# Keys of the next batch ahead of the values, and the value copy and loads at the head of ScalarE's next step, in the attention stage of a gated layer

## The chip, the core and the metric

The kernel runs on one core of a Trainium2 chip. The metric is the device time of one execution in microseconds; lower is better. Engines: PE is TensorE (PEld its weight loads), DVE is VectorE, ACT is ScalarE, POOL is GpSimd, SP is SyncE. SPq, ACTq and POOLq in the rows are the same engines' queues issuing DMA transfers.

## The reference

Two residual blocks. The first is a decayed linear attention with rotary factors, the second a two-of-eight mixture of experts whose weights each have a low-rank correction.

```
q, k, v = LN(x) @ Wq, ctx @ Wk, ctx @ Wv            # 8 batches of 256 x 256
q, k = xpos(q), xpos(k)                             # rotary, with a scale
ret  = (q @ k.T) * decay_mask
x    = x + tanh(g_xattn) * (ret @ v)
xf   = LN(x)
gates = top-2 of softmax(xf @ Wg.T), normalised
y_e  = (silu(xf @ (W1 + A1 B1) + b1) * (xf @ (W3 + A3 B3) + b3)) @ (W2 + A2 B2) + b2   # 8 experts
x    = x + tanh(g_ffn) * sum_e gates_e * y_e
```

## The kernel before

All engine programs are written out by hand, each in the order in which its engine runs it; semaphores join them. There are two stages. The first runs eight steps, one per batch of 256 rows, and the change lies in it. The second works through 39 tiles of 128 gathered rows, one expert each, and its matmuls follow one another with hardly a gap.

In step `s` of the first stage three things are interleaved. For batch `s`: the key, query and value projections, their rotation, the layer norm of the input rows. For batch `s-1`: scores, the masked product with the values, the residual, the second layer norm. For batch `s-2`: the expert logits and the two largest. Beside them the weights of expert `s-1` are made ready: `unit(s-1, ., m)`, m = 0 to 5, is a sixth of the low-rank product on PE, `add` puts it on a staged sixth of the weight on DVE, `weight_hi` (`hi(m)`) rounds that on ACT into WH, and `weight_lo` on POOL writes the rest into WL, which frees the staging buffer for SP's next load.

The names that the steps below use:

- PE `step`: the key product into `pK`; transposes of `xn2` (normalised rows of batch `s-2`); `scores(s)`; `units(0, 1)`; `logits(s-2)`, which wait for ACT's copy `xn2T`; `attend`, which waits for DVE's masked `ret` and for the copy `v`; transposes of `xn`; `units(2, 3)`; the query product, which waits for ACT's copy `xnT`; the value product into `pV`; `units(4, 5)`.
- DVE `step`: rotation of the keys in two products (`tA`, `tB`), the variance between them; then a reciprocal (`rs`) that waits for ACT's square root `sd` of that variance; shift, mask, adds 0 and 1, the two largest, residual, adds 2 and 3 and the second norm between them; rotation of the queries; sums of the next rows; adds 4 and 5.
- ACT `step`: copy `xn2T`, square root `sd`, normalised rows `xn`, `hi(0, 1)`, copy `xnT`, `hi(2)`, second square root, `hi(3)`, normalised rows `xn2`, value copy `v`, two DMA stores (`out`, `xn_rows`), two DMA loads by `next_batch(s+2)` (rows `xs`, context `cx`), `hi(4, 5)`, and in steps 1 to 3 a store of low-rank factors (`lora_parts`).

The rows `xs` have three buffers, the context `cx` two. The context buffer is read by the key product and by the value product of its batch, so its reload stands behind a wait for the value product on ACT.

Of the kernel before, what the change touches and what calls it, by code (L numbers as in the profile page):

```python
# [31 lines left out]
ACT = mybir.ActivationFunctionType  # L32
# [3 lines left out]
B, S, D = 8, 256, 256  # L36
# [44 lines left out]
def flamingo(nc, x, ctxT, wqkv, tables, mask, gates_in, w_all, lora, biases, wgT, ident_in, consts, out):  # L81
# [9 lines left out]
    with whole:  # L91
# [379 lines left out]
        def _(pe):  # L471
# [9 lines left out]
            def unit(s, u, m):  # L481

                kind, n = m // 2, s * UNITS + m
                lb, before = ls_of(s, kind)
                if m % 2 == 0:
                    pe.wait_ge(s_ls[lb], 3 * 16 * (s + 1 if lb == kind else E + 1))
                pos_wait(pe, s_add, n - 1)
                L = LS[lb]
                if kind < 2:
                    c = m % 2  # L490
                    last = nc.tensor.matmul(pW[m % 2][:, :], L[:, c * P:(c + 1) * P], L[:, D:LCOL], start=True, stop=True)
                else:
                    for h in range(2):
                        c = 2 * (m % 2) + h
                        last = nc.tensor.matmul(pW[m % 2][:, h * D:(h + 1) * D], L[:, c * P:(c + 1) * P], L[:, HID:LCOL],
                                                start=True, stop=True)
                last.then_inc(s_unit, 1)
# [36 lines left out]
                nc.tensor.matmul(pO[:, D:2 * D], ret[:, 2 * P:3 * P], vv[:, 1, :], start=False, stop=True  # L534
                                 ).then_inc(s_out, 1)

            def step(s, u, two, three):
                def units(*ms):
                    if two:
                        for m in ms:  # L540
                            unit(s - 1, 1 - u, m)

                pe.wait_ge(s_ctx[u], 16 * (half(s, u) + 1))
                pos_wait(pe, s_krot, s)
                for m in range(2):
                    for c in range(CH):
                        last = nc.tensor.matmul(pK[:, m * S:(m + 1) * S], wq[:, 1, c, m * P:(m + 1) * P], cx[u][:, c, :],
                                                start=(c == 0), stop=(c == CH - 1))
                last.then_inc(s_kproj, 1)
                if three:  # L550
                    pe.wait_ge(s_xn2, s - 1)
                    transposes(xn2, s_xn2Tp)
                if two:
                    scores(s)
                units(0, 1)
                if three:
                    pe.wait_ge(s_qrot, s)
                    logits(s - 2, pL)
                if two:
                    attend(s, v[1 - u])  # L560
                else:
                    pe.wait_ge(s_vtab, 2 * 16)
                if three:
                    pe.wait_ge(s_xn2T, s - 1)
                pe.wait_ge(s_xn, s + 1)
                transposes(xn, s_xnTp)
                units(2, 3)
                if not two:
                    pe.wait_ge(s_tab, 4 * 16)
                pe.wait_ge(s_xnT, s + 1)  # L570
                pos_wait(pe, s_qrot, s)
                pos_wait(pe, s_L, s - 1)
                for m in range(2):
                    for c in range(CH):
                        last = nc.tensor.matmul(pQ[:, m * S:(m + 1) * S], wq[:, 0, c, m * P:(m + 1) * P], xnT[:, c, :],
                                                start=(c == 0), stop=(c == CH - 1))
                last.then_inc(s_qproj, 1)

                pos_wait(pe, s_v, s)
                for t in range(TPB):  # L580
                    for c in range(CH):
                        last = nc.tensor.matmul(pV[:, t * D:(t + 1) * D], cx[u][:, c, t * P:(t + 1) * P], wq[:, 2, c, :],
                                                start=(c == 0), stop=(c == CH - 1))
                last.then_inc(s_vproj, 1)
                if s == B - 1:
                    ranks(1, pK, trimA, onesA, HA, HSA)
                units(4, 5)

            def ranks(n, dst, tri, ones, H, HS):

# [133 lines left out]
        def _(act):  # L724
# [25 lines left out]
            def weight_hi(s, u, m):  # L750
                act.wait_ge(s_add, s * UNITS + m + 1)
                nc.scalar.activation(w_dst(WH, s, m), stage[stage_of(s * UNITS + m)][:, :], ACT.Copy).then_inc(s_wh, 1)  # L752
# [18 lines left out]
            def next_batch(t, u):  # L771

                r = t % XRING
                pos_wait(act, s_x2, t - XRING + 1)
                act.dma_start(xs[r][:] if r < 2 else xs[r], x[t]).then_inc(s_xload[r], 16)
                act.dma_start(cx[u][:], ctxT[t]).then_inc(s_ctx[u], 16)

            def store_rows(b):

                rows = bass.ds(b * S, S)  # L780
                act.wait_ge(s_x2, b + 1)
                act.wait_ge(s_xn2, b + 1)
                if b < B - 1:
                    act.dma_start(out_rows[rows, 0:D].rearrange("(t p) d -> p t d", p=P), x2[:]).then_inc(s_store, 16)
                act.dma_start(xn2_d[rows, 0:D].rearrange("(t p) d -> p t d", p=P), xn2[:]).then_inc(s_store, 16)
# [13 lines left out]

            def step(s, u, two, three):  # L800
                hi = lambda *ms: [weight_hi(s - 1, 1 - u, m) for m in ms]
                if three:
                    act.wait_ge(s_xn2Tp, s - 1)
                    copy_xn2T(pT)
                act.wait_ge(s_mv1, s + 1)
                nc.scalar.activation(sd1[:], mv1[:, :, 1], ACT.Sqrt, bias=eps_t[:]).then_inc(s_sd1, 1)
                act.wait_ge(s_nm1, s + 1)
                pos_wait(act, s_xnTp, s)
                normal(xs[s % XRING], rs1, nm1, xn, s_xn)
                if two:  # L810
                    hi(0, 1)
                if three:
                    first_two(s - 2)
                act.wait_ge(s_xnTp, s + 1)
                nc.scalar.activation(xnT[:].rearrange("p c t -> p (c t)"), pT[:, :], ACT.Copy).then_inc(s_xnT, 1)
                if s == 0:
                    round_factors()
                    pair_factors()
                if s == B - 2:
                    act.wait_ge(s_cst, 16)  # L820
                    act.wait_ge(s_lstore, 3 * 16)
                    nc.scalar.activation(trimA, cst[:, C_TRI:C_TRI + P], ACT.Copy, scale=1.0, bias=-1.0).then_inc(s_fixed, 1)
                    nc.scalar.activation(onesA, cst[:, C_TRI:C_TRI + P], ACT.Copy, scale=0.0, bias=1.0).then_inc(s_fixed, 1)
                    nc.scalar.activation(HA, cst[:, C_TRI:C_TRI + P], ACT.Copy, scale=0.0, bias=0.0).then_inc(s_fixed, 1)
                    nc.scalar.activation(F9, cst[:, C_E:C_E + E + 1], ACT.Copy, scale=0.0, bias=0.0).then_inc(s_fixed, 1)
                    nc.scalar.activation(c5, cst[:, C_E:C_E + E], ACT.Copy, scale=float(SPARE), bias=float(SPARE)).then_inc(s_fixed, 1)
                    nc.scalar.activation(kj1, cst[:, C_HI:C_HI + KJ], ACT.Copy, scale=float(P), bias=float(P)).then_inc(s_fixed, 1)
                if s == B - 1:
                    nc.scalar.activation(slots_x, cst[:, C_IOTA:C_IOTA + P].unsqueeze(2).to_broadcast([P, P, KQ]), ACT.Copy
                                         ).then_inc(s_grid, 1)  # L830
                if two:
                    hi(2)
                    deviation(s - 1)
                    hi(3)
                    if s == B - 1:
                        act.wait_ge(s_dl, 1)
                        nc.scalar.activation(e2A, dlA, ACT.Exp).then_inc(s_e2, 1)
                        act.wait_ge(s_e2, 1)
                        nc.scalar.activation(denA, e2A, ACT.Copy, scale=1.0, bias=1.0).then_inc(s_e2, 1)
                    act.wait_ge(s_nm2, s)  # L840
                    normal(x2, rs2, nm2, xn2, s_xn2)
                act.wait_ge(s_vproj, s + 1)
                nc.scalar.activation(v[u][:].rearrange("p t d -> p (t d)"), pV[:, :], ACT.Copy).then_inc(s_v, 1)
                if two:
                    store_rows(s - 1)
                if s + 2 < B:
                    next_batch(s + 2, u)
                if two:
                    if s < B - 1:
                        hi(4, 5)  # L850
                    if s <= 3:
                        store_factors(s - 1)
# [760 lines left out]
```

## Time and profile before

| what | value |
|---|---|
| three runs | 329.84, 327.46, 328.63 us; median 328.63 us |
| span of the profiled execution (first to last instruction) | 325.4 us |
| PE busy | 297.9 us (92%) |
| DVE, ACT, POOL busy | 248.2, 206.0, 210.8 us |
| mean granted TensorE clock | 0.975 |

The time of the profiled execution itself isn't listed apart; its span lies 3.2 us under the median of the runs, and a run's time takes in what lies around the span. Busy shares are averages over two stages with different limits; the first stage is the stretch up to about 105 us.

### The profile page before, as it was taken

To read this page: it belongs to the slowest core of one execution; us is meant where nothing else is said; L and a number is where in the kernel's file an instruction comes from. 1 tells how busy PE (TensorE), PEld (TensorE's weight loads), DVE (VectorE), ACT (ScalarE), POOL (GpSimd) and SP (SyncE) were. 2 spreads that over 40 slices of the span, in tenths; PEclk is the share of its full clock that TensorE was granted. 3 is DMA by queue.
4 is the path that set the end of the run, shared out by engine and by line. 5 is a ranking of instruction groups with operands and counts; after the bars stand their busy time and mean duration, and the time that the engine had idled before them with its cause. 6 is when DMAs were issued, how large, how long until landed. Compare 5 with 4: busy or idle time off the path is not lost. (4 is left out here: it accounts for less than half of the span.)

```text
span 325.4 us, 7435 instructions
## 1 busy us (share of the span) xinstructions
PE 297.9 (92%) x1755; PEld 230.0 (71%) x1755; DVE 248.2 (76%) x607; ACT 206.0 (63%) x486; POOL 210.8 (65%) x246
## 2 busy tenths in 40 slices
PE   7589989999997798999999999999999999999960
PEld 3468778788886656776777777777777777777740
DVE  2679879889999998697988976767776776777750
ACT  5635755766878577787675565665675665675550
POOL 2457878888893098866756656766577776666241
PEclk9799999999999699999999999999999999999996
DMA  7968997999972169567747675766533223333100
GB/s 265 391 158 240 280 297 253 294 279 278 278 244 85 17 225 296 138 201 200 205 139 206 175 187 186 175 187 197 148 56 55 52 51 66 53 45 61 20 0 0
DMA packets 30424, 54.35 MB, mean 167 GB/s; under 512 B 7232, under 2 KB 15808, under 8 KB 30112
## 3 DMA queue, kind: packets, MB, share of 16 engines
q1 hardware_dynamic: 14672, 36.10, 34.1%
q0 software_dynamic: 7488, 9.36, 16.7%
q10 hardware_dynamic: 8224, 8.42, 8.6%
q8 instruction: 17, 0.28, 0.4%
q14 instruction: 23, 0.19, 0.2%
HBM read 41.92 MB, written 10.65 MB: 162 GB/s over the span
## 5 line engine op out<-in xcount | busy, mean ns | idle before, releaser
L1079 POOL DMA_INDIRECT out<-ys,cols x39 | 64.7, 1660 | 58.4 <-DMA out<-ys,cols 33.0
L883 ACT ACTIVATE gh<-bank 128x512 fp32r<-128x512 f32 x39 | 23.4, 599 | 61.0 <-PE bank L648 61.0
L640 PE MATMUL bank<-WH,xh 128*128 x156 | 55.7, 438 | 0.1
L1056 POOL DMA_INDIRECT xg<-xn_rows,colg x39 | 40.0, 1026 | 20.5 <-POOL colg L1034 10.3
L992 POOL TENSOR_TENSOR WL<-stage,WH 128x512 bf16<-128x512 f32 x38 | 47.9, 1278 | 7.3 <-ACT WH L752 7.1
L640 PE MATMUL bank<-WH,xl 128*128 x156 | 49.0, 395 | 0.0
L640 PE MATMUL bank<-WL,xb 128*128 x156 | 47.2, 385 | 0.0
L752 ACT ACTIVATE WH<-stage 128x512 fp32r<-128x512 f32 x38 | 22.9, 628 | 17.7 <-DVE stage L1110 14.5
L640 PEld LDWEIGHTS bank<-WH,xl 128*128 128x128 f32 x156 | 29.2, 188 | 6.8 <-DVE xl L1493 0.4
L1497 DVE TENSOR_TENSOR gl<-bank,gh 128x512 fp32r<-128x512 f32 x39 | 26.9, 689 | 8.8 <-ACT gh L883 8.7
L657 PE MATMUL bank<-WH,gh 128*128 x156 | 32.0, 327 | 1.5 <-ACT gh L883 1.5
L1509 DVE TENSOR_TENSOR g<-g,h 128x512 f32<-128x512 f32 x39 | 27.1, 694 | 5.0 <-ACT h L945 1.1
L1503 DVE TENSOR_TENSOR h<-bank,BA 128x512 f32<-128x512 f32 x23 | 15.9, 691 | 19.3 <-PE bank L640 18.1
L657 PEld LDWEIGHTS bank<-WH,gh 128*128 128x128 f32 x156 | 24.0, 190 | 7.7 <-issue 2.7
L1110 DVE TENSOR_TENSOR stage<-bank,stage 128x512 f32<-128x512 f32 x38 | 24.6, 676 | 0.9 <-DMA stage<-w_all_in 0.9
L657 PE MATMUL bank<-WH,gl 128*128 x156 | 24.9, 281 | 0.4 <-DVE gl L1497 0.4
L640 PEld LDWEIGHTS bank<-WH,xh 128*128 128x128 f32 x156 | 24.0, 190 | 1.7 <-issue 0.7
L648 PEld LDWEIGHTS bank<-ident,g 128*128 128x128 f32 x156 | 19.3, 140 | 8.1 <-DVE g L1509 1.1
L887 ACT ACTIVATE gb<-gh 128x512 bf16<-128x512 f32 x39 | 24.9, 638 | 0.0
L945 ACT ACTIVATE h<-h 128x512 f32<-128x512 f32 x39 | 24.9, 638 | 0.0
L640 PEld LDWEIGHTS bank<-WL,xb 128*128 128x128 bf16 x156 | 9.0, 98 | 21.3 <-issue 21.3
L657 PE MATMUL bank<-WL,gb 128*128 x156 | 23.8, 275 | 0.0
(229 smaller groups left out, 702.2 us busy)
## 6 DMA issues: line engine op xcount, KB each, us to landing
BB<-biases_in SPq DMA_DIRECT2D x16, 640.0 KB, 4.1
stage<-w_all_in SPq DMA_DIRECT2D x38, 256.0 KB, 5.1
BA<-biases_in SPq DMA_DIRECT2D x8, 640.0 KB, 3.9
WL<-w_all_in SPq DMA_DIRECT2D x10, 256.0 KB, 4.7
LS<-WH SPq DMA_DIRECT2D x45, 48.0 KB
xn_rows<-xn ACTq DMA_DIRECT2D x8, 256.0 KB, 4.1
out<-x ACTq DMA_DIRECT2D x7, 256.0 KB, 3.1
cx<-ctxT_in ACTq DMA_DIRECT2D x6, 256.0 KB, 6.5
```

What stands on the lines that cost most here:

```text
L640: last = nc.tensor.matmul(dst[:, :], lhs[p][:, c * P:(c + 1) * P], W[:, bass.ds(e * (UNITS * UC) + (2 * kind + c) * UC, HID)], start=(part ...
L657: last = nc.tensor.matmul(pY[:, 0:D], lhs[:, c * P:(c + 1) * P], W[:, bass.ds(e * (UNITS * UC) + 4 * UC + c * D, D)], start=(part == 0 and ...
L752: nc.scalar.activation(w_dst(WH, s, m), stage[stage_of(s * UNITS + m)][:, :], ACT.Copy).then_inc(s_wh, 1)
L883: nc.scalar.activation(gh[:], pG[:, :], ACT.Copy).then_inc(s_gh, 1)
L887: nc.scalar.activation(gb[:], gh[:].bitcast(F32), ACT.Copy).then_inc(s_gb, 1)
L945: nc.scalar.activation(h1[:], h1[:], ACT.Silu).then_inc(s_silu, 1)
L992: nc.gpsimd.tensor_tensor(w_dst(WL, s, m), stage[stage_of(s * UNITS + m)][:, :], w_dst(WH, s, m).bitcast(F32), ALU.subtract).then_inc(s_wl, 1)
L1056: nc.gpsimd.indirect_dma_start(out=xg[q][:], out_offset=None, in_=xn2_d[0:JA * P, :] if i < NA else xn2_d, in_offset=bass.IndirectOffsetOn ...
L1079: nc.gpsimd.indirect_dma_start(out=out_rows, out_offset=bass.IndirectOffsetOnAxis(ap=cols[:, i:i + 1], axis=0), in_=ys[p][:], in_offset=No ...
L1110: nc.vector.tensor_tensor(stage[b][:, :], pW[m % 2][:, :], stage[b][:, :], ALU.add).then_inc(s_add, 1)
L1497: nc.vector.tensor_tensor(gl[:], pG[:, :], gh[:].bitcast(F32), ALU.subtract).then_inc(s_gl, 1)
L1509: nc.vector.tensor_tensor(g[:], g[:], h1[:], ALU.mult).then_inc(s_g, 1)
```

## The change

PE's key product becomes a function `keys`. Step 0 runs it for batch 0 at its head as before; every step but the last then runs `units(4, 5)` and the key product of the next batch between its query and its value product. On ACT the value copy of a batch and the two loads move from the end of a step to the head of the next, behind `hi(4, 5)` and the factor store and ahead of the copy `xn2T`; the loads are for the batch after the one of that step, `next_batch(s+1)`. The last step keeps its value copy and its units where they were. DVE, POOL and SP run the same programs.

```diff
-            def step(s, u, two, three):
-                def units(*ms):
-                    if two:
-                        for m in ms:
-                            unit(s - 1, 1 - u, m)
+            def keys(s, u):
 
                 pe.wait_ge(s_ctx[u], 16 * (half(s, u) + 1))
                 pos_wait(pe, s_krot, s)
...
                 last.then_inc(s_kproj, 1)
+
+            def step(s, u, two, three):
+                def units(*ms):
+                    if two:
+                        for m in ms:
+                            unit(s - 1, 1 - u, m)
+
+                if s == 0:
+                    keys(0, 0)
                 if three:
                     pe.wait_ge(s_xn2, s - 1)
                     transposes(xn2, s_xn2Tp)
...
                 last.then_inc(s_qproj, 1)
+                if s < B - 1:
+                    units(4, 5)
+                    keys(s + 1, 1 - u)
 
                 pos_wait(pe, s_v, s)
...
                 if s == B - 1:
                     ranks(1, pK, trimA, onesA, HA, HSA)
-                units(4, 5)
+                    units(4, 5)
...
+            def copy_values(b, u):
+                act.wait_ge(s_vproj, b + 1)
+                nc.scalar.activation(v[u][:].rearrange("p t d -> p (t d)"), pV[:, :], ACT.Copy).then_inc(s_v, 1)
+
...
                 hi = lambda *ms: [weight_hi(s - 1, 1 - u, m) for m in ms]
+                if two:
+                    copy_values(s - 1, 1 - u)
+                    if s + 1 < B:
+                        next_batch(s + 1, 1 - u)
                 if three:
                     act.wait_ge(s_xn2Tp, s - 1)
                     copy_xn2T(pT)
...
-                act.wait_ge(s_vproj, s + 1)
-                nc.scalar.activation(v[u][:].rearrange("p t d -> p (t d)"), pV[:, :], ACT.Copy).then_inc(s_v, 1)
+                if s == B - 1:
+                    copy_values(s, u)
                 if two:
                     store_rows(s - 1)
-                if s + 2 < B:
-                    next_batch(s + 2, u)
                 if two:
                     if s < B - 1:
                         hi(4, 5)
```

On PE, in a middle step, from the units 2 and 3 (L491) over the query product (first L575, now L580), the value product (L582, now L590), units 4 and 5 (L495) and the next key product (L547, now L543) to the transposes (L502):

```order
 L491 MATMUL bank<-LS 128x512 x2
-L575 MATMUL bank<-xnT,wq 128x256 x4
-L582 MATMUL bank<-wq,cx 128x256 x4
+L580 MATMUL bank<-xnT,wq 128x256 x4
 L495 MATMUL bank<-LS 128x256 x4
-L547 MATMUL bank<-cx,wq 128x256 x4
+L543 MATMUL bank<-cx,wq 128x256 x4
+L590 MATMUL bank<-wq,cx 128x256 x4
 L502 MATMUL bank<-ident,xn 128x128 x4
```

The value product went from the place before the units to the last place before the transposes; the units and the key product stand one product earlier.

On ACT, from the normalised rows `xn2` (the row xn<-x) at the end of step 3 to the square root `sd` at the head of step 4, in the kernel before (WL<-x_in loads rows into the third rows buffer, which lies in WL):

```order
L757 ACTIVATE xn<-x,nm,rs 128x256 x2
L843 ACTIVATE v<-bank 128x512
L784 DMA out<-x 128x2x256
L785 DMA xn_rows<-xn 128x2x256
L775 DMA WL<-x_in 128x512
L776 DMA cx<-ctxT_in 128x512
L752 ACTIVATE WH<-stage 128x512 x2
L736 DMA lora_parts<-WH 48x2304
L769 ACTIVATE xn2T<-bank 128x512
L806 ACTIVATE sd<-mv,eps_t 128x2
```

And in the changed kernel, the same stretch with the loads of the same batch:

```order
L765 ACTIVATE xn<-x,nm,rs 128x256 x2
L796 DMA out<-x 128x2x256
L797 DMA xn_rows<-xn 128x2x256
L760 ACTIVATE WH<-stage 128x512 x2
L744 DMA lora_parts<-WH 48x2304
L788 ACTIVATE v<-bank 128x512
L783 DMA WL<-x_in 128x512
L784 DMA cx<-ctxT_in 128x512
L777 ACTIVATE xn2T<-bank 128x512
L822 ACTIVATE sd<-mv,eps_t 128x2
```

The value copy and the two loads went from ahead of the two roundings (WH<-stage) to behind them and behind the factor store, right ahead of the copy `xn2T` and the square root.

## Rows read from the trace of the kernel before

**Rows 1.** Stretches, steps 5 and 6: busy PE, PEld, DVE, ACT, POOL; clock; DMA share; GB/s

```profile
66.28:78.28 12.00, 11.49 (x65) 9.72 (x63) 10.81 (x36) 7.97 (x18) 10.47 (x11) 1.00 1.02 300
78.28:89.91 11.63, 11.32 (x65) 9.80 (x64) 10.61 (x36) 8.90 (x24) 10.31 (x11) 1.00 0.90 265
```

**Rows 2.** Timeline of DVE (start, length, instruction, idle before): first reciprocal of a step

```profile
21.37 0.15 DVE L1137 RECIPROCAL rs<-sd 128x2 f32<-128x2 f32 x1
...
58.36 0.17 DVE L1137 RECIPROCAL rs<-sd 128x2 f32<-128x2 f32 x1 [0.76 <-ACT sd L806]
...
70.36 0.17 DVE L1137 RECIPROCAL rs<-sd 128x2 f32<-128x2 f32 x1 [0.73 <-ACT sd L806]
...
81.98 0.17 DVE L1137 RECIPROCAL rs<-sd 128x2 f32<-128x2 f32 x1 [0.35 <-ACT sd L806]
...
93.17 0.15 DVE L1137 RECIPROCAL rs<-sd 128x2 f32<-128x2 f32 x1
```

**Rows 3.** Timeline of ACT, from the end of step 4 into step 5

```profile
66.01 0.60 ACT L843 ACTIVATE v<-bank 128x512 f32<-128x512 f32 x1
66.07 0.42 ACTq L784 DMA_DIRECT2D out<-x  x1
...
67.05 0.57 ACTq L775 DMA_DIRECT2D xs<-x_in  x1
67.65 0.82 ACTq L776 DMA_DIRECT2D cx<-ctxT_in  x1
68.51 1.15 ACT L752 ACTIVATE WH<-WL 128x512 fp32r<-128x512 f32 x2 [1.91 <-DVE WL L1110]
69.57 0.58 ACT L769 ACTIVATE xn2T<-bank 128x512 f32<-128x512 f32 x1
70.05 0.28 ACT L806 ACTIVATE sd<-mv,eps_t 128x2 f32<-128x2 f32 x1
```

**Rows 4.** Timeline of PE, step 5: query, value, units 4 and 5, next keys, transposes

```profile
74.25 1.99 PE L575 MATMUL bank<-xnT,wq 128*128 128x256 f32 x8 [0.31 <-ACT xnT L815]
76.08 1.89 PE L582 MATMUL bank<-wq,cx 128*128 128x256 f32 x8
77.62 0.82 PE L495 MATMUL bank<-LS 128*128 128x256 f32 x4
78.28 1.89 PE L547 MATMUL bank<-cx,wq 128*128 128x256 f32 x8
80.00 0.60 PE L502 MATMUL bank<-ident,xn 128*128 128x128 f32 x4
```

**Rows 5.** Timeline of DVE: adds 4 and 5 in step 5; key rotation in step 7

```profile
78.60 1.27 DVE L1110 TENSOR_TENSOR stage<-bank,stage 128x512 f32<-128x512 f32 x2
...
91.83 0.69 DVE L1115 TENSOR_TENSOR tA<-bank,WH 128x512 f32<-128x512 f32 x1 [0.34 <-PE bank L547]
```

**Rows 6.** Timeline of ACT: other value copies and loads, in steps 0, 2 and 5

```profile
17.58 0.60 ACT L843 ACTIVATE v<-bank 128x512 f32<-128x512 f32 x1 [2.81 <-PE bank L582]
17.59 0.36 ACTq L775 DMA_DIRECT2D WL<-x_in  x1
17.98 0.45 ACTq L776 DMA_DIRECT2D cx<-ctxT_in  x1
...
42.70 1.41 ACTq L776 DMA_DIRECT2D cx<-ctxT_in  x1
...
79.03 0.52 ACTq L775 DMA_DIRECT2D xs<-x_in  x1
79.58 0.50 ACTq L776 DMA_DIRECT2D cx<-ctxT_in  x1
```

**Rows 7.** Tile view of the context buffers

```profile
DMA to landing us min/median/max: 3.3/6.4/7.5
```

**Rows 8.** DMA view: issues, count, KB each, median us to landing

```profile
cx<-ctxT_in ACTq DMA_DIRECT2D x6, 256.0 KB, 6.5
lora_parts<-WH ACTq DMA_DIRECT2D x3, 432.0 KB, 7.0
```

## The prediction

> **What bounds the kernel now.** I read the page first for the two stages, then the first stage step by step in the view of stretches, then the timelines of DVE, ACT and PE side by side through one step. The second stage is one row of matmuls and nothing of it is touched, so what the first stage gains or loses is what the kernel gains or loses. So PE has about 0.3 to 0.5 us of slack a step, and something else makes the step long.
>
> That is a loop through DVE and ACT. I measure it at the first reciprocal of a step, where DVE waits 0.73 to 0.76 us for ACT's square root [rows 2]: from 58.36 to 70.36 is 12.00 us, from 70.36 to 81.98 is 11.62, and from 21.37 to 93.17 are six loops, 71.80 us together. Read one loop backwards from 70.36 [rows 2, 3]. The square root starts at 70.05, right behind the copy xn2T (69.57), which stands behind the two roundings (68.51). ACT's engine stood idle for 1.91 us ahead of them while its queue was issuing: four DMAs from 66.07 to 68.47, that is 2.40 us, of which 0.98 (66.07 to 67.05) are the two stores and 1.42 (67.05 to 68.47) the two loads. So the loop is 7.71 us from the reciprocal to the first store (66.07 - 58.36), then 2.40 of issue, then 1.89 (68.47 to 70.36: 0.04, two roundings 1.06, copy 0.48, square root 0.31). Issue time on ACT counts fully in it.
>
> **The change, part by part.** I put the reciprocal of step 5 (70.36) at zero and lay the moved work on it.
>
> *PE.* Queries start at +3.89 (74.25), and take 1.83 to the next product; values 1.54, units 4 and 5 0.66, keys 1.72 (from start to start in [rows 4]). Now units start at +5.72, keys at +6.38, values at +8.10, and the last value matmul ends at +8.10 + 1.89 = +9.99. PE's total is unchanged, and the transposes behind start at the same +9.64. The keys 1.54 us earlier are worth little: DVE waited for them 0.34 us [rows 5], but in a loop whose reciprocal then waits for ACT anyway, except in the last (93.17 has no wait behind it).
>
> *ACT, roundings.* Stores now follow the normalised rows directly and are over at about 67.0. The roundings then wait for adds 4 and 5 alone, which end at +9.51 (78.60 + 1.27 - 70.36) [rows 5]. That removes 2.40 us of issue ahead of them and puts DVE's own row of queries, sums and adds in its place.
>
> *ACT, value copy and loads.* Both now stand between the roundings and the copy xn2T. The copy of the values itself costs nothing where loads follow: it runs on the engine while the queue issues (66.01 and 66.07 [rows 3]). But its wait counts, because what is queued behind it is the loads, the copy xn2T and the square root, for which PE's logits and DVE's reciprocal wait. Values end at +9.99, later than the roundings' release at +9.51, so the copy starts at +10.03 (0.04 behind its release, as the roundings do now), the first load at +10.09; with D for the issue of the two loads, xn2T starts at +10.13 + D, the square root 0.48 later, the reciprocal 0.31 after that. The loop becomes **10.92 + D**.
>
> In steps 1 to 3 the factor store is issued ahead of the copy as well, about 0.5 us from +9.6; it ends near +10.1, with the values, and adds 0.1 or nothing.
>
> *What is D?* Before it was 0.84 with nothing else in the queue (17.59 to 18.43), 1.05 (79.03 to 80.08), 1.42 (67.05 to 68.47); in step 2 the context load alone took 1.41, some 0.9 more than in step 5 [rows 3, 6]. The bounds are 0.84 and 1.42, with a long issue on top. The changed loads no longer come directly behind two stores, which speaks for the low end; SP's weight loads fall in the same time as they do now, which speaks against it. I take 1.1, next to the 1.05 of step 5.
>
> *The last loop* (step 6 to 7) has no loads before or after, but gains a value copy ahead of xn2T: 0 to 0.53 us (one step of two roundings), less the 0.34 that keys come earlier. It took 93.17 - 81.98 = 11.19; I take 11.4.
>
> *Sum.* Five loops of 10.92 + 1.1 and one of 11.4 make 71.5, against 71.80: 0.3 us gained, 325.1 of span for 325.4, and **328.3 us** against the median of 328.63. At D = 0.84 it is 70.2 (327.0), at 1.42 73.1 (329.9), with one long issue 0.9 more. The change takes the issue of two stores and two roundings out of the loop and puts adds, the wait for later values and the same loads in; the two are worth the same. As the three runs spread over 2.4 us, under 1% (3.3 us) can't be told from nothing.
>
> **Covers.** The loads come later against their use. The context load's issue starts about 1.4 us ahead of a step's reciprocal (its own 0.55, then 0.04, 0.48 and 0.31), and the keys that read it now start at +6.38 of that same step: 7.8 us. Landing took 3.3 to 7.5, median 6.4 [rows 7]: covered, by 0.3 in the worst row. The rows are issued first and are read only shortly ahead of adds 4 and 5 (+8.24). The stores are issued no later than before, and the roundings 4 and 5, for which POOL waits, come earlier.
>
> **Rivals.**
>
> *Keys wait for their context (slower).* In steps 1 to 3 the factor store of 432 KB (7.0 us to landing [rows 8]) now goes ahead of the loads in the same queue, where it went behind them. Four transfers of the size of the context's, 256 KB [rows 8], took about 8.0 us from the first issue to the median landing of the context (67.65 + 6.4 - 66.07), 128 KB per us; 432 more are 3.4 us. Then the context lands 11.4 us after the first store, which is issued at -4.3, so at +7.1, 0.7 late, and with the longest landing 1.8 late. PE then holds the keys, and with them the values, on which the loop hangs directly. Three loops with 0.7 to 1.8 are 2.1 to 5.4 us; I put it at 331. Against it: in its present place, last of the five and issued about with the roundings (68.51, 1.85 ahead of 70.36), the store lands 7.0 us later at some +5.2, and the bytes ahead of the last of the five are the same in any order. It decides from where a landing takes more than 7.8 us.
>
> *Long issues hit the loads.* A 1.41 like that of step 2 in two or three loops instead of one: 0.9 each, 329.5 to 331.5.
>
> *The loads don't wait for the copy (faster).* If the queue could issue a DMA while an instruction ahead of it still waits for its semaphore, the loads would be out of the loop; it would be the copy behind two roundings, +9.54 + 1.06 + 0.48 + 0.31, 11.4 us in all loops, 68.4 against 71.80: 325.2. The trace speaks against it: in step 0 the engine idles 2.81 us before the value copy, and the load behind it, which waits for nothing of its own, starts 0.01 us after the copy (17.59) and not in that idle time [rows 6]. The Trainium skill, page "Perfetto Trace Analysis", section "Per-instruction lifecycle: what the profiler-reported window actually captures", has it the other way: an ACT instruction is pushed with its semaphore wait into a wait queue and the sequencer goes on to the next one. By that rule the time is the 325.2 of this rival; the trace at 17.59 disagrees.
>
> *The change doing nothing at all* is the forecast's neighbour and not told apart from it: the orders are fixed, so it does what it says.
>
> **How the numbers follow.** Forecast (D between 0.84 and 1.42) 0.62: 328.3, own range 327.0 to 329.9. Context late 0.19: 331, half of it over 331.9. Long issues 0.12: some 330.5, rarely over 331.9. Loads free 0.07: 325.2. The range of 326.2 to 331.6 leaves out the last case and the top of the second, and takes in a bad long issue. Faster by over 1% (under 325.3): the last case and a little of the forecast's low end, 0.09. Slower (over 331.9): half of the context case and a little of the long issues, 0.13. Within 1%: 0.78.
>
> **What the profile would show.** Right: PE waits nowhere for DMA; the roundings 4 and 5 start with DVE's adds; the loads start 0.06 behind the value copy and that with the end of the value product; the reciprocal still waits for ACT, 0.8 to 1.3 us; loops of 11.8 to 12.4. Wrong: an idle row of PE's keys ended by a DMA of cx; loops of 11.4 with loads issued ahead of the copy; or issue rows of the pair well under 0.8 or over 1.5 us.

## The result

The changed kernel takes 338.2 us (median of 4 runs, 336.59 to 341.44), the kernel before 328.76 on the same chip: a ratio of 1.0286, 95% interval 1.0231 to 1.0341. It is slower by 9.4 us, where 328.3 was forecast with a range up to 331.6. Each profile below is of one execution, and some are the longest that their kernel had (341.44 us for the changed kernel, with a span of 339.6), so times and ratios are taken from the medians and the profiles are read for their first stage.

The stretches of the changed kernel between the first reciprocals of its steps, in the columns of [rows 1]: length; busy time of PE, PEld, DVE, ACT, POOL; granted clock; DMA share; GB/s.

```profile
21.70:37.11 15.41, 12.88 (x63) 10.40 (x61) 10.00 (x28) 7.86 (x15) 11.67 (x12) 0.92 0.67 179
37.11:53.30 16.19, 13.26 (x64) 10.89 (x64) 10.62 (x35) 8.28 (x17) 10.25 (x10) 0.89 0.83 234
53.30:68.57 15.27, 13.22 (x64) 10.84 (x64) 10.63 (x35) 8.28 (x17) 10.26 (x10) 0.89 0.73 212
68.57:80.20 11.63, 11.12 (x61) 9.59 (x62) 10.60 (x34) 7.99 (x17) 7.46 (x7) 1.00 0.84 257
80.20:92.87 12.67, 11.51 (x63) 9.84 (x62) 10.51 (x34) 8.09 (x17) 11.48 (x12) 1.00 0.92 276
92.87:104.23 11.36, 11.05 (x64) 9.58 (x62) 10.51 (x35) 8.86 (x23) 8.98 (x10) 1.00 0.82 247
```

The six loops add up to 82.53 us; before it was 71.80 [rows 2]. Three of them carry 9.9 of the 10.7 us, at 15.3 to 16.2 us each. They are the ones in which a factor store is issued (steps 1 to 3, at 32.21, 48.30 and 63.76); the other three are 11.4 to 12.7. In the three long ones the granted clock is below 1.00 as well.

The timeline of DVE shows what those three wait for, at the rows that answer to [rows 2].

```profile
37.11 0.17 DVE L1151 RECIPROCAL rs<-sd 128x2 f32<-128x2 f32 x1 [3.62 <-ACT sd L822]
53.30 0.17 DVE L1151 RECIPROCAL rs<-sd 128x2 f32<-128x2 f32 x1 [4.11 <-ACT sd L822]
68.57 0.17 DVE L1151 RECIPROCAL rs<-sd 128x2 f32<-128x2 f32 x1 [3.60 <-ACT sd L822]
80.20 0.17 DVE L1151 RECIPROCAL rs<-sd 128x2 f32<-128x2 f32 x1 [0.57 <-ACT sd L822]
```

The wait for the square root was 0.73 to 0.76 us; it is 3.6 to 4.1 now. The timeline of ACT in front of the second of these, and then in front of the fourth, answers to [rows 3]:

```profile
48.30 0.33 ACTq L744 DMA_DIRECT2D lora_parts<-WH  x1
48.68 0.60 ACT L788 ACTIVATE v<-bank 128x512 f32<-128x512 f32 x1 [0.16 <-issue]
48.71 0.81 ACTq L783 DMA_DIRECT2D xs<-x_in  x1
49.55 2.89 ACTq L784 DMA_DIRECT2D cx<-ctxT_in  x1
52.48 0.60 ACT L777 ACTIVATE xn2T<-bank 128x512 f32<-128x512 f32 x1 [3.20 <-issue]
...
78.42 0.35 ACTq L783 DMA_DIRECT2D xs<-x_in  x1
78.81 0.53 ACTq L784 DMA_DIRECT2D cx<-ctxT_in  x1
78.87 0.58 ACT L788 ACTIVATE v<-bank 128x512 f32<-128x512 f32 x1
```

The context load's issue alone lasts 2.89 us, and `xn2T` and the square root stand behind it: "3.20 <-issue" is ScalarE with work ready and its queue still issuing. Without the factor store (78.42) the pair is issued in 0.92 us. The pair's issue, from the first load's start to the second's end, is 3.63, 3.73 and 3.27 us in the three loops with a store, and 0.92 and 0.84 in the two without.

SyncE stalls in the same moments. Its timeline in the changed kernel, around the first and the third store:

```profile
28.62 1.05 SPq L382 DMA_DIRECT2D stage<-w_all_in  x2
...
31.54 4.68 SPq L382 DMA_DIRECT2D stage<-w_all_in  x2
...
63.70 3.94 SPq L382 DMA_DIRECT2D WL<-w_all_in  x2
```

Two weight loads take 1.05 us to issue, and 4.68 and 3.94 beside the stalled loads of ScalarE. Both ends lie within 0.1 us of the end of ScalarE's pair (36.22 and 36.25, 67.64 and 67.70). The first of the two loads at 31.54 was long by itself, 1.67 us, and it began ahead of the factor store (32.21) and behind the two row stores (30.34 and 30.81), so the factor store isn't all that stands behind these stalls.

### The profile page after: what moved, and what is told of

Its sections match the earlier page's. It is cut to its first block and busy times, and to the rows that moved or that the text cites. A ratio compares the mean times of both kernels' runs of the same rounds, so it can differ in the third digit from the quotient of the medians.

```text
span 339.6 us, 7435 instructions
## 1 busy us (share of the span) xinstructions
PE 303.6 (89%) x1755; PEld 233.9 (69%) x1755; DVE 248.9 (73%) x607; ACT 206.8 (61%) x486; POOL 209.6 (62%) x246
## 5 line engine op out<-in xcount | busy, mean ns | idle before, releaser
L1093 POOL DMA_INDIRECT out<-ys,cols x39 | 63.3, 1624 | 61.5 <-DMA out<-ys,cols 38.5
L1523 DVE TENSOR_TENSOR g<-g,h 128x512 f32<-128x512 f32 x39 | 27.9, 716 | 4.9 <-ACT h L959 0.6
L1529 DVE SCALAR_TENSOR_TENSOR ys<-bank,gsel,ys 128x256 f32<-128x256 f32 x39 | 18.8, 483 | 9.4 <-ACT ys L943 7.8
L656 PE MATMUL bank<-ident,g 128*128 128x128 f32 x156 | 23.6, 274 | 0.3 <-DVE g L1523 0.3
```

What stands on the lines that cost most here:

```text
L656: last = nc.tensor.transpose(pG[:, c * P:(c + 1) * P], g[:, c * P:(c + 1) * P], ident[:])
L1093: nc.gpsimd.indirect_dma_start(out=out_rows, out_offset=bass.IndirectOffsetOnAxis(ap=cols[:, i:i + 1], axis=0), in_=ys[p][:], in_offset=No ...
L1523: nc.vector.tensor_tensor(g[:], g[:], h1[:], ALU.mult).then_inc(s_g, 1)
```

## The experiments

In the runs below, a loop is the time between first reciprocals, and D is the issue time of the two loads as the prediction defines it. Ratios are to the kernel before on the same chip, with their 95% intervals.

### Is it the place of the factor store?

Two theories: the loads stall because the factor store stands right ahead of them; or they stall because they fall into a crowded moment of SyncE's transfers, wherever the store is. First, the changed kernel with the store behind the normalised rows of the next step:

```
 normal(xs[s % XRING], rs1, nm1, xn, s_xn)
+if 2 <= s <= 4:
+    store_factors(s - 2)
...
 hi(4, 5)
-if s <= 3:
-    store_factors(s - 1)
```

> The changed kernel with the three factor stores issued behind the loads: behind the normalised rows of the next step, instead of ahead of its value copy. Theory S (the loads' issue stalls because the factor store was issued right ahead of them): the issue of the two loads falls from 3.3 to 3.7 us to about 0.9 to 1.2 in those three loops, the loops to 11.8 to 12.2 us, TensorE's clock stays at 1.00 there, 327 to 330 us. Theory T (the loads stall because they now fall on a crowded moment of SP's transfers, wherever the store stands): the stalls stay, 335 to 341 us.

Measured: 329.14 us against 331.35, ratio 0.9934 (0.9894 to 0.9974). D is 0.84, 1.04, 1.43, 1.56 and 1.01, the loops 11.46 to 12.56, 72.67 together. Moving one DMA takes away the whole loss.

Second, the kernel before, with nothing changed but the store, which goes ahead of its loads:

```
 store_rows(s - 1)
+if s <= 3:
+    store_factors(s - 1)
 if s + 2 < B:
     next_batch(s + 2, u)
...
-if s <= 3:
-    store_factors(s - 1)
```

> The kernel before with one thing changed: the three factor stores are issued ahead of the two loads instead of behind the roundings. Theory S: the issue of the loads grows by 1.5 to 2.7 us in three steps, and with it three loops, and the clock may fall in them: 333 to 339 us. Theory T: the loads' issue moves by no more than the store's own 0.5 us: 328.5 to 330.5 us.

Measured: 342.22 us, ratio 1.0307 (1.0211 to 1.0403). Its ACT timeline, step 1:

```profile
30.62 0.75 ACTq L736 DMA_DIRECT2D lora_parts<-WH  x1
31.41 0.54 ACTq L775 DMA_DIRECT2D xs<-x_in  x1
31.98 2.31 ACTq L776 DMA_DIRECT2D cx<-ctxT_in  x1
34.34 1.15 ACT L752 ACTIVATE WH<-stage 128x512 fp32r<-128x512 f32 x2 [4.16 <-issue]
```

The three context loads take 2.31, 2.21 and 2.86 us. So the store's place alone makes the kernel before as slow as the change did, with the old order of everything else. A part of that is again the clock: the stretches from 36.19 to 84.65 us show 0.80, 0.80 and 0.76. The theory of a crowded moment falls as a cause by itself.

### What the two halves of the change are worth

ScalarE's part alone: the changed kernel with TensorE's program of before.

```
-if s == 0:
-    keys(0, 0)
+keys(s, u)
...
-if s < B - 1:
-    units(4, 5)
-    keys(s + 1, 1 - u)
...
-    units(4, 5)        # in the last step alone
+units(4, 5)            # behind the values, in every step
```

> The changed kernel with PE's order of before (values ahead of units 4 and 5, keys at the head of the step); ACT's program as changed. Both theories keep the stalled loads in three loops. The value copy's release moves from +9.99 to about +7.6, so the loop hangs on the roundings' release at +9.54 and becomes 10.43 + D, 0.49 less; the 0.85 us that PE's keys waited for their context goes: 2 to 4 us under the changed kernel, 333 to 336 us. If the early keys are worth something by themselves, it is slower than the changed kernel instead, over 339 us.

Measured: 335.43 us, ratio 1.0153 (1.0076 to 1.023). The three context loads still take 2.08, 2.21 and 2.35 us; the loops are 14.54, 14.78, 14.94 and then 11.57, 11.37, 11.40.

TensorE's part alone: the kernel before with units 4 and 5 and the next keys ahead of the values.

```
 last.then_inc(s_qproj, 1)
+if s < B - 1:
+    units(4, 5)
+    keys(s + 1, 1 - u)
...                        # at their old places only in the last and the first step
```

> The kernel before with TensorE's part of the change alone: units 4 and 5 and the next keys ahead of the values; ScalarE as before. Theory of the loop: the value copy, and behind it stores, loads and roundings, then wait for the end of the values at +9.99; 10.09 + 2.40 of issue + 1.89 make 14.4 for a loop with loads and 12.96 for the last, together 13.8 us more than the 71.80 of before, a ratio of about 1.042. Rival: what counts is ScalarE's issue time, and TensorE's order costs only the 0.5 us a loop seen between the changed kernel and the one with the old order; then 1.01.

Measured: 346.92 us, ratio 1.0515 (1.042 to 1.061). Its stretches:

```profile
22.21:36.88 14.67, 11.38 (x60) 9.15 (x58) 9.90 (x28) 7.79 (x15) 9.00 (x9) 1.00 0.77 232
36.88:52.87 15.99, 13.30 (x64) 10.91 (x64) 10.63 (x35) 8.09 (x17) 10.25 (x11) 0.89 0.73 218
52.87:67.05 14.18, 11.63 (x64) 9.73 (x64) 10.51 (x34) 7.97 (x17) 10.26 (x11) 1.00 0.78 242
67.05:82.41 15.36, 13.11 (x64) 10.84 (x64) 10.71 (x35) 8.09 (x17) 10.25 (x11) 0.89 0.75 220
82.41:98.89 16.48, 14.63 (x64) 12.09 (x64) 10.71 (x35) 8.08 (x17) 10.24 (x11) 0.79 0.65 193
98.89:113.12 14.23, 13.22 (x64) 10.88 (x64) 10.61 (x34) 8.99 (x23) 10.25 (x11) 0.88 0.63 193
```

The loop arithmetic said 14.4, and the two loops at full clock are 14.67 and 14.18. The next three are above it by 1.0 to 2.1 us, the last, put at 12.96, by 1.3, and in all four the granted clock is below 1.00. The rival with the 0.5 us a loop falls. The wait for the values counts in full as soon as stores, loads and roundings are queued behind the copy, which is why the two parts of the change belong together.

Both repairs at once, the old order on TensorE and the store behind the loads:

> Both: PE's order of before, and the factor stores behind the loads; of the change only the value copy and the loads at the head of ScalarE's next step are left. Theory S: loops of 10.43 + D with D near 1.0, that is 11.4 to 11.6 us instead of 12.0: 325 to 328 us, a little faster than before. Theory T: as without the moved store, 333 to 336 us.

Measured: 328.01 us, ratio 0.9892 (0.9843 to 0.9942), D 0.84 to 1.47, loops 11.36 to 12.32.

### What of the store makes the loads stall?

The changed kernel with each store cut into halves of the columns; one half ahead of the loads, or both. A third version issues the whole store from GpSimd.

```
-act.dma_start(lora_rows[:, part, :], ...)
+act.dma_start(lora_rows[:, part, h * w:(h + 1) * w], ...)      # w: half of the columns
...
 hi(4, 5)
-    store_factors(s - 1)
+    store_factors(s - 1, 0)       # and (s - 1, 1): here, or behind the normalised rows of the next step
```

> The changed kernel with each factor store cut into two stores of half the columns (216 KB): one stays ahead of the loads, the other goes behind the normalised rows of the next step. If the stall grows with the bytes that stand ahead, D's excess over 1.0 is halved: D 2.1 to 2.4 in the three loops, ratio about 1.015. If any store of this shape stalls what follows, by its 48 long rows and not by its bytes: D 3.3 to 3.7 as in the changed kernel, 1.028. If there is a limit which only the whole store passes: D 0.9 to 1.4, ratio about 0.995.

> The changed kernel with each factor store cut into two stores of half the columns, both ahead of the loads: the same 432 KB in the same place, in smaller pieces. If the loads stall because so many bytes stand ahead of them in the queue: D (from the first load's issue to the end of the second's) 2.3 to 3.7 in the three loops, or the second half's own issue stalls in its place, ratio 1.02 to 1.03. If it is the size of one store: D 0.9 to 1.6 with some 0.4 more of issue for the second half, ratio about 1.00.

With one half ahead: ratio 1.0003 (0.9911 to 1.0096), D 1.39, 1.61 and 0.96. With both ahead: ratio 1.0309 (1.0242 to 1.0376), D 2.52, 2.98 and 2.37. The ACT timelines in step 3, first of the one and then of the other:

```profile
57.75 0.33 ACTq L745 DMA_DIRECT2D lora_parts<-WH  x1
...
58.43 0.36 ACTq L785 DMA_DIRECT2D WL<-x_in  x1
58.82 0.57 ACTq L786 DMA_DIRECT2D cx<-ctxT_in  x1
```

```profile
61.28 1.36 ACTq L745 DMA_DIRECT2D lora_parts<-WH  x2
...
62.71 1.01 ACTq L785 DMA_DIRECT2D WL<-x_in  x1
63.74 1.34 ACTq L786 DMA_DIRECT2D cx<-ctxT_in  x1
```

It is not one large DMA that is harmful: from the first piece's issue to the end of the second load the two pieces took 3.61, 4.02 and 3.80 us, and the whole store in the changed kernel 4.04, 4.14 and 3.94. The stall is only spread over more rows (second half, rows, context). Half of the bytes cost little, 0.3 us of D on average over 1.0, where a share in proportion was expected to cost 1.1 to 1.4; its D lies hardly outside the 0.84 to 1.56 of the kernel with the whole store behind. I read it as a limit on what may be outstanding, but as a limit on the amount alone the trace of before speaks against that. At its start SyncE issues loads without a pause, and the last of them are these six weight loads:

```profile
7.75 3.01 SPq L382 DMA_DIRECT2D stage<-w_all_in  x6
```

That is 0.5 us each, although at 10.29 twelve earlier loads, some 2600 KB, hadn't landed. Those are loads alone, on one queue; where issues stall, stores are among them and two queues issue. Which of the two matters no run here separates.

Nor is the factor store the only thing that counts. In the kernel before the pair of step 2 took 2.20 us (41.91 to 44.11) and kept the roundings waiting, when the last factor store had landed at 38.4; the two row stores stood ahead of it, as they do in these versions too, and what they add was not tested.

The store issued by GpSimd:

```
 rotated(qT, s_qT)
+if two and s <= 3:
+    store_factors(s - 1)          # pool.dma_start
```

> The changed kernel with the factor store issued by GpSimd, behind its rotated queries, about 0.4 us ahead of where ScalarE issued it. If the loads stall because they stand behind the store in ScalarE's own queue: D back to 0.9 to 1.4, ratio about 0.995. If the store fills something that all queues share (SyncE's issues stalled together with ScalarE's): D 2.5 or more still, and SyncE's issues stall beside them; ratio 1.015 to 1.03.

Measured: 330.38 us, ratio 1.0028 (0.9942 to 1.0115). D is 0.89, 2.54 and 0.85. Its timelines of ACT and then of SyncE at the middle store, which GpSimd issued at 43.37:

```profile
44.83 0.35 ACTq L775 DMA_DIRECT2D xs<-x_in  x1
45.53 1.84 ACTq L776 DMA_DIRECT2D cx<-ctxT_in  x1
47.42 0.60 ACT L769 ACTIVATE xn2T<-bank 128x512 f32<-128x512 f32 x1 [2.00 <-issue]
...
43.59 3.71 SPq L382 DMA_DIRECT2D stage<-w_all_in  x2
```

Two loops of three are free of the stall, one is not, and in that one SyncE stalls with ScalarE again. So ScalarE's own queue is not the whole of it, and what holds the issues up is shared at least in part; which resource it is stays open.

### What the lower clock costs

The three long loops of the changed kernel are above 10.92 + D, by 0.86, 1.54 and 1.08 us (the expectation below says 0.96 for the first, but 15.41 less 14.55 is 0.86). The timeline of PE, from the start of each of the three and of the loop after them:

```profile
20.41 2.59 PE L513 MATMUL bank<-qT,kT 128*128 128x256 f32 x8 [2.61 <-POOL qT L1012]
...
37.04 1.15 PE L523 MATMUL bank<-wg,xn2T 128*128 128x8 f32 x8 [2.32 <-ACT xn2T L777]
38.23 1.22 PE L532 MATMUL bank<-v,ret 128*128 128x256 f32 x2
...
53.18 1.03 PE L523 MATMUL bank<-wg,xn2T 128*128 128x8 f32 x8 [2.67 <-issue]
...
68.45 1.03 PE L523 MATMUL bank<-wg,xn2T 128*128 128x8 f32 x8 [1.84 <-issue]
69.69 0.70 PE L532 MATMUL bank<-v,ret 128*128 128x256 f32 x2 [0.20 <-DVE ret L1198]
```

Behind waits of 2.32 and 2.67 us in front of the logits, which the stalled loads cause, follow the stretches with 0.89; at 38.23 the attend product takes 1.22 us. Behind the wait of 1.84 us it takes 0.70 and its stretch has 1.00. The first loop's 0.92 lies behind another wait, 2.61 us for GpSimd's rotated queries in step 1, and that one comes and goes: the first loop shows 0.91, 0.87 and 0.89 in three of the other profiles, where this wait is 2.62 to 2.70 us (the old order on TensorE, the same with the store behind, the store from GpSimd), and 1.00 in all others, where it is 1.1 us or less.

The length of a wait doesn't settle the clock by itself. With the old order on TensorE the waits in front of the logits are 1.46, 1.46 and 1.45 us, and the stretches behind them show 0.88, 0.89 and 1.00. With TensorE's part alone a stretch behind a wait of 2.53 us shows 1.00. With half of the store ahead the third stretch shows 0.87 behind a wait of 0.73 us.

The experiment keeps PE at work in the wait in front of the logits, with products whose result is overwritten, in steps 2 to 4:

```
 if three:
+    if s <= 4:
+        pe.wait_ge(s_x2, s - 1)
+        keep_clock(5, wq[:].rearrange("p a c d -> p (a c d)"), pO)      # the second version: 2
     pe.wait_ge(s_qrot, s)
     logits(s - 2, pL)
```

> The changed kernel with five products more on TensorE (128x512, of the weights with themselves, their sum overwritten) in its wait ahead of the logits, in the three loops with a factor store. Theory: what these loops took above 10.92 + D (0.96, 1.54 and 1.08 us) is TensorE at the lower granted clock behind that wait. Then the attend product keeps 0.6 to 0.7 us instead of 1.06 to 1.22, the stretch shows 1.00, the three loops come to 10.92 + D (about 14.3 to 14.6, with D still 3.3 to 3.7), and the time falls by 2.5 to 3.5 us against the changed kernel, to a ratio of about 1.019. Rival: the excess is late work of VectorE and ScalarE, whatever the clock; then the clock is 1.00 and the ratio stays at 1.028.

Measured: 341.19 us, ratio 1.0338 (1.0263 to 1.0413), granted clock 1.00 in all six loops, and no gain. The five products took 4.45 us, longer than the wait, and themselves held the logits up. It tells nothing between the theories. With two:

> As the kernel with five products in TensorE's wait ahead of the logits, with two in their place: five took 4.45 us, longer than the wait of 2.3 to 2.7 us, so that they held up the logits themselves; two take 1.8. Theory (the loops' excess over 10.92 + D comes from the lower granted clock behind the idle wait): granted clock 1.00 in the loops from the first reciprocal of step 2 on, and the second and third loop within 0.4 us of 10.92 + D, where the changed kernel had 1.54 and 1.08 more; D stays at 2 to 3.7, ratio about 1.02. Rival: the excess is work that comes late whatever the clock; then the clock is 1.00 and the excess stays above 1.

Measured: 335.64 us, ratio 1.0146 (1.0098 to 1.0195). Its stretches:

```profile
21.11:35.47 14.36, 13.11 (x64) 9.89 (x62) 9.92 (x29) 7.98 (x15) 11.67 (x12) 1.00 0.79 218
35.47:49.51 14.04, 13.38 (x68) 10.52 (x68) 10.51 (x34) 8.17 (x17) 10.10 (x10) 1.00 0.89 261
49.51:63.94 14.43, 13.34 (x68) 10.47 (x68) 10.52 (x34) 8.05 (x17) 10.44 (x11) 1.00 0.85 242
```

D is still 2.93, 2.83 and 3.54 us, so 10.92 + D is 13.85, 13.75 and 14.46. In the second and the third loop, which begin with the filled wait, the excess is now 0.29 and -0.03, for 1.54 and 1.08 in the changed kernel: the clock's share is real, above 1 us in each. The value product shows where it lies. The timelines of PE in the second loop, of the changed kernel and of this version:

```profile
46.40 1.89 PE L590 MATMUL bank<-wq,cx 128*128 128x256 f32 x8
...
43.39 1.89 PE L593 MATMUL bank<-wq,cx 128*128 128x256 f32 x8
```

The values were to end 9.99 us behind the reciprocal. They end 11.18 us behind it in the changed kernel (48.29 - 37.11) and 9.81 here (45.28 - 35.47); in the third loop it is 11.09 and 9.82. Not all of the shorter time is the clock's: D, too, is smaller in this profile, 9.30 us in the three loops together for 10.63, and nothing here shows why.

The first loop begins ahead of all filling; its clock is 1.00 in this run anyway, and of its excess of 0.51 the store's own issue explains the greater part (1.08 us in place of some 0.34).

### The loads where ScalarE waits anyway

If issue time in front of the roundings is what the loop consists of, the loads belong where ScalarE waits anyway. This is the kernel before with its loads and the store behind the copy `xnT`, and in a second version with the context load behind the first square root:

```
 copy xnT
+if two and s + 1 < B:
+    load_context(s + 1, 1 - u)     # second version: behind the square root sd1
+if s + 2 < B:
+    load_rows(s + 2)
+if 2 <= s <= 4:
+    store_factors(s - 2)
...
-if s + 2 < B:
-    next_batch(s + 2, u)
```

> The kernel before with its loads and the factor store taken out of the end of the step and put behind the copy of the transposed normalised rows, where ScalarE waits 1.2 us for VectorE's adds: the context of the next batch, the rows of the one after, then the factor store. TensorE's order as before. If issue time ahead of the roundings is what the loop consists of (1.42 of its 2.40 us gone): loops of about 11.4, which is what VectorE and TensorE need by themselves, 68.4 for 71.80, ratio about 0.99. If the loads stall there, or the copy's place is on the loop too: above 12 a loop, ratio 1.00 or more.

Measured: 329.38 us, ratio 0.9955 (0.9921 to 0.9988). Loops 11.28, 11.26, 11.57, 12.12, 12.79, 11.44. In the two long ones the keys wait for their context, 0.42 and 1.08 us; the timeline of PE:

```profile
76.90 1.99 PE L547 MATMUL bank<-cx,wq 128*128 128x256 f32 x8 [1.08 <-DMA cx<-ctxT_in]
```

> The kernel with the loads in ScalarE's pause, with the context load alone moved 3.9 us earlier, right behind the square root, where ScalarE waits 0.69 us for VectorE (its issue took 0.35 us in the pause). There the context was issued only about 5 us ahead of the keys, and in two loops TensorE waited for it, 0.42 and 1.08 us (loops of 12.12 and 12.79; the others 11.26 to 11.57). If that is all that kept these two long: no wait of the keys for the context, all six loops at 11.3 to 11.6, together 68.4 for 71.80 of before, ratio 0.988 to 0.991. If a long issue there holds up the normalised rows behind it: loops over 12, ratio 0.995 or more.

Measured: 326.55 us against 331.55, ratio 0.9896 (0.9831 to 0.9961). No key product waits for a context; the loops are 11.09, 11.45, 11.98, 11.64, 11.22 and 12.30, together 69.68. The ratio is the one expected, but the loops are not all at 11.4: in the stretch of 12.30 PE is busy for 11.83, so by then PE's own work is close to being the bound. This version and the one with both repairs can't be told apart by time.

## Why the prediction was wrong

**The step that failed** is "What is D?" together with "In steps 1 to 3 the factor store is issued ahead of the copy as well, about 0.5 us ...; it ends near +10.1, with the values, and adds 0.1 or nothing". The store was priced at its own issue. What it does to the issue behind it was not priced at all. D was put at 1.1, with bounds of 0.84 to 1.42; behind the store it is 3.63, 3.73 and 3.27. That is 7.3 us more than three times 1.1. Moving the store back behind the loads, and moving it ahead of them in the kernel before, shows this cause from both sides.

The bound was wrong because all the issue rows that I used are of ScalarE, where before the change nothing followed the store closely. Of these rows the choice of 1.1 also left out some: the pairs of before were 1.36, 2.20, 1.46, 1.42 and 1.05 us in steps 1 to 5, 1.50 on average. On SyncE issues did follow the store, and the trace of before has them. In it ScalarE issued the store at 31.43, 44.61 and 56.64. The timeline of SyncE in the kernel before, three factor loads of a kind in each row (away from a store, behind the first store, ahead of the second, behind the second, behind the third):

```profile
25.04 1.78 SPq L373 DMA_DIRECT2D LS<-WH  x3
...
33.32 2.47 SPq L373 DMA_DIRECT2D LS<-WH  x3
...
41.34 2.74 SPq L373 DMA_DIRECT2D LS<-WH  x3
...
45.28 3.44 SPq L373 DMA_DIRECT2D LS<-WH  x3
...
58.38 2.97 SPq L373 DMA_DIRECT2D LS<-WH  x3
```

Three loads took 1.78 us where nothing held them up, and 2.47, 3.44 and 2.97 within two us behind a store. But it was 2.74 ahead of the second store, too, in the same moment as ScalarE's context load of 1.41 [rows 6] (they end at 44.08 and 44.11), and 2.83 at 62.76, 6 us behind the third. So issues that stall on both queues were there to be seen, with a store and without; the prediction took the 1.41 for one "long issue" and didn't ask what it depends on. In these steps of the kernel before no wait of TensorE ended with a DMA, so on SyncE it cost nothing; I read the store only on the engine that issued it. The prediction's own sign of being wrong, a pair "well under 0.8 or over 1.5 us", is what came.

**The second missing term** is the clock. The forecast took the granted clock of 1.00 from [rows 1] for granted. In the long loops it was 0.92, 0.89 and 0.89, and they are 0.86, 1.54 and 1.08 us above the formula. For the second and the third the two filling products show the cause, PE's wait behind the stalled loads. The first lies behind a wait of step 1 that has no tie to the loads, and for it there is only a comparison. In the profiles of the store behind, of half a store ahead, of both halves ahead and of the store from GpSimd the sixteen loops with loads at a clock of 1.00 lie between -0.30 and +0.61 us of 10.92 + D, and the four at 0.87 to 0.89 lie +0.79 to +1.73 above it.

**What held.** The formula of 10.92 + D: without the store the loops are 11.63 (11.84 by the formula with its D of 0.92) and 12.67 (11.76 with 0.84). The 0.9 us more in the second of these is "Keys wait for their context": the timeline of PE has

```profile
87.41 2.00 PE L543 MATMUL bank<-cx,wq 128*128 128x256 f32 x8 [0.85 <-DMA cx<-ctxT_in]
```

The longest landing of a context rose from 7.5 us [rows 7] to 8.6, beyond the 7.8 from which this rival decides. It came once, and not in a loop with a store, where the same stall delays the keys too; it is 0.9 of the loss, not the 3.4 a loop of shared bandwidth that the rival worked out. The last loop was put at 11.4 and is 11.36. That the wait of the value copy counts because of what is queued behind it held as well: with TensorE's part alone the copy waits in front of the stores too, and the time is 5% up.

The terms add up, against the 71.5 of the forecast: D behind the store +7.33, the excess of those three loops +3.48, the other D's -0.44, what the two other loops are off by -0.21 and +0.91, the last -0.04; together 11.03, and 82.53 were measured.

**"The loads don't wait for the copy"** did not happen. At 91.17 ScalarE idled 0.64 us for the values, and copy and first load start together at its end, as at 17.59 before. The rule of the Trainium skill, page "Perfetto Trace Analysis", section "Per-instruction lifecycle: what the profiler-reported window actually captures", by which the queue goes on past a waiting instruction, disagrees with this trace as well. At 78.42 the first load did start ahead of the copy (78.87), but there the values had ended at 78.38, and the copy waited only for its engine, not for a semaphore.

**What stays open.** The profiled execution of the changed kernel is 3.1 us longer than that of before after the last of these reciprocals, too (339.6 - 104.23 = 235.4 against 325.4 - 93.17 = 232.2 us). The same stretch lasts from 231.4 to 236.5 us in the other profiles whatever their first stage, so I don't put it down to the change. And why the issue stalls is known only in part, since more bytes than these were outstanding at the start without a stall. 432 KB of factor store ahead on the same queue bring it every time, in one DMA or in two, and 216 KB hardly do; but issued from GpSimd the 432 KB brought it in one loop of three, and the kernel before had a pair of 2.20 us without them.

## What to carry to other kernels

A DMA issue has no fixed price: on an engine that also computes, look at what stands ahead of it in the queue, and at how long issues on every queue last behind that same transfer in the trace at hand. Issue large stores last, behind whatever the engine's next instruction needs, and put loads where the engine waits anyway, but check how much time that leaves them until their reader. A stall that leaves TensorE idle can be paid twice, since the products behind it may run at the lower clock.

## What the runs showed of the hardware

- Behind a 432 KB store, two loads of 256 KB took 3.3 to 3.7 us to issue in place of 0.84 to 0.92, and issues of SyncE beside them were long too and ended with them (two weight loads 4.68 us in place of 1.05). The Trainium skill, page "DMA: Bandwidth & Descriptors", section "Issuing engines are not separate DMA queues", says that all issuing engines share the same DMA engines, which fits the common stall; it calls the time to initiate a DMA usually small beside the DMA, and here a context load took 2.89 us of issue out of the 7.41 us from the start of its issue to its landing.
- With 216 KB of factor store ahead D was 0.96 to 1.61 us, hardly more than the 0.84 to 1.56 with the store behind the loads; with twice 216 KB it was 2.37 to 2.98. No threshold follows: without the store a pair took 2.20 us in the kernel before.
- After waits of 2.32 and 2.67 us TensorE ran part of the next products at the lower of its two clock levels: the stretch of 38.20 to 41.00 us shows a granted clock of 0.50, the attend product 1.22 us in place of 0.70. After a wait of 1.84 us it did not; in other versions stretches behind waits of 1.46 us showed 0.88 and 0.89, and one behind 2.53 us showed 1.00, so the length of the wait alone doesn't say it. With two filling products in the wait, the granted clock stayed at 1.00 in the loops behind it.
